# A hybrid Mamba, attention and FFN layer on eight cores: half of the scan's input products on GpSimd, FFN weights through two buffers, attention weights read from unpacked arrays

## The reference

```python
x = x + mamba(layernorm(x))
x = x + ffn(layernorm(x))
x = x + attention(layernorm(x))
x = x + ffn(layernorm(x))          # the same FFN weights again

# mamba: 2048 inner channels d, 16 states n, 2048 steps t
xb, zb = silu(conv4(h @ Wx)), silu(h @ Wz)
dt, B, C = x_proj(xb); dt = softplus(dt @ dt_proj)
decay[t,d,n] = exp(dt[t,d] * A[d,n])
inp[t,d,n]   = dt[t,d] * B[t,n] * xb[t,d]
h[t] = decay[t] * h[t-1] + inp[t]
y[t,d] = sum_n h[t,d,n] * C[t,n]
out = ((y + xb * D) * zb) @ out_proj

# ffn: weights become alpha * sign(w), alpha = mean |w| of a row
# attention: for every token its 16 heads of 64 attend to one another, then Wo
```

## Time and profile before

| | |
|---|---|
| median of the 2 runs | 6503.46 us (6502.35 to 6504.58) |
| the profiled execution, its own time | 6548.37 us |
| span of that execution, slowest core (core 7) | 6546.8 us (6480.4 to 6546.8 over the cores) |
| TensorE busy in the span | 2947.1 us (45%) |
| VectorE busy | 3181.0 us (49%) |
| ScalarE busy | 1508.9 us (23%) |
| GpSimd busy | 351.3 us (5%) |

### The profile page before, as it was taken

One profiled execution on the slowest core, in us unless ns is written; L12 is line 12 of the kernel. 1 busy time (PEld: TensorE's weight loads), 2 busy tenths in 40 slices (PEclk: granted clock), 3 DMA queues, 4 the chain that ended last, 5 costly groups with the idle time before them and its releaser, 6 DMA issues.

```text
span 6546.8 us, 37208 instructions; the slowest of 8 cores (6480.4 to 6546.8 us)
## 1 busy us (share of the span) xinstructions
PE 2947.1 (45%) x10144; PEld 1174.4 (18%) x10144; DVE 3181.0 (49%) x2980; ACT 1508.9 (23%) x2890; POOL 351.3 (5%) x204
## 2 busy tenths in 40 slices
PE   2323224322242322422224777879533443347978
PEld 1100001000010000100001444534211111113433
DVE  0267783577845778558885000010355556552011
ACT  1133331233322333223332222221100010001120
POOL 0000000000000000000000000000022222220000
PEclk9655557655575555665556666778766666668989
DMA  5300003100010000110001112211200000001213
GB/s 111 81 12 10 2 0 77 36 12 5 0 52 34 11 8 0 39 39 0 0 0 37 53 58 77 90 49 62 51 0 0 0 0 0 0 0 37 74 49 111
DMA packets 88973, 209.50 MB, mean 32 GB/s; under 512 B 32314, under 2 KB 32445, under 8 KB 83776
## 3 DMA queue, kind: packets, MB, share of 16 engines
q1 hardware_dynamic: 71584, 159.75, 7.6%
q0 software_dynamic: 17184, 47.37, 3.5%
HBM read 191.40 MB, written 37.88 MB: 35 GB/s over the span
## 4 chain that ended last, share of the span: by engine, by line
DVE 34%; PE 34%; ACT 11%; issue 9%; DMA 5%; DVEq 4%; ACTq 2%; POOL 1%; SPq 0%; POOLq 0%
DVE AR L739 18%; PE ps L982 8%; PE ps L1065 8%; ACT AR L717 5%; DVE AR L1213 4%; PE ps L478 3%; DVEq L58 3%; DVE AR L1249 3%; PE ps L1276 2%; DVE AR L519 2%; PE ps L314 2%; PE ps L1180 2%; PE ps L960 2%; ACTq L58 1%; POOL AR L1262 1%
## 5 line engine op out<-in xcount | busy, mean ns | idle before, releaser
L763 PE MATMUL ps<-AR 128*128 128x512 bf16 x1024 | 517.8, 608 | 1939.9 <-DVE AR L755 1939.9
L739 DVE TENSOR_TENSOR_SCAN AR<-AR 128x1024 bf16<-128x1024 f32 x512 | 1173.3, 2292 | 135.9 <-ACT AR L723 124.6
L1082 DVE TENSOR_SCALAR AR<-ps,AR 128x1024 f32<-128x1024 f32 x32 | 43.0, 1344 | 1333.3 <-ACT AR L1077 684.5
L717 ACT ACTIVATE AR<-AR 128x511 f32<-128x511 f32 x1024 | 675.4, 707 | 1.4 <-issue 1.1
L982 PE MATMUL ps<-AR 128*128 128x512 bf16 x2048 | 552.8, 441 | 84.2 <-DVE AR L349 84.2
L1276 PE MATMUL ps<-AR 128*128 128x512 bf16 x512 | 220.2, 586 | 635.8 <-POOL AR L1262 609.2
L1065 PE MATMUL ps<-AR 128*128 128x512 bf16 x2048 | 497.8, 410 | 4.7 <-ACT AR L994 4.7
L763 PEld LDWEIGHTS ps<-AR 128*128 128x128 bf16 x1024 | 70.2, 104 | 2379.0 <-issue 2379.0
L748 ACT ACTIVATE AR<-AR 128x2 f32<-128x2 bf16 x512 | 105.3, 206 | 1351.3 <-DVEq L63 1351.3
L755 DVE TENSOR_TENSOR AR<-AR 128x1024 bf16<-128x1024 bf16 x512 | 354.2, 692 | 125.4 <-issue 125.4
L478 PE MATMUL ps<-AR 128*128 128x512 bf16 x1024 | 308.7, 464 | 149.3 <-DVE AR L349 66.1
(11 more groups left out here) (102 smaller groups left out, 2559.4 us busy)
## 6 DMA issues: line engine op xcount, KB each, us to landing
AR<-ip_bf SPq DMA_DIRECT2D x96, 256.0 KB, 2.6
AR<-w2s SPq DMA_DIRECT2D x48, 512.0 KB, 3.6
AR<-bc_hbm SPq DMA_DIRECT2D x4, 4096.0 KB, 14.3
AR<-w2pk SPq DMA_DIRECT2D x16, 1024.0 KB, 6.2
AR<-op_bf SPq DMA_DIRECT2D x24, 512.0 KB, 3.6
AR<-w1s SPq DMA_DIRECT2D x48, 256.0 KB, 2.6
AR<-w1s POOLq DMA_DIRECT2D x48, 256.0 KB, 2.9
X<-x_fm SPq DMA_DIRECT2D x1, 8192.0 KB, 29.6
```

Source lines behind the costliest of these rows:

```text
L717: nbase=nbase: e.activation(out=dec_all[gb][:, n, 1:TQ], in_=dt[b][:, 1:TQ], func=AF.Exp, scale=av[:, dd, nbase + n:nbase + n + 1]))
L739: e.tensor_tensor_scan(out=h_all[hb].rearrange("p a b -> p (a b)"), data0=dec_all[gb].rearrange("p a b -> p (a b)"), data1=inp_all[ib].rea ...
L763: e.matmul(self.bank(b, TQ), self.ident[:], hc_all[hb][:, n, :], start=(ng == 0 and n == 0), stop=(ng == NG - 1 and n == G - 1)),
```

## The change

There are three parts.

**Scan.** For odd ng the input product no longer runs on VectorE but on GpSimd (new line 735; for even ng it stays on VectorE, new line 744). GpSimd waits for the scan of group ng-2 (its output buffer is that scan's input) and for vdup; VectorE's scan of the odd group waits for GpSimd's event in addition to ScalarE's. The prologue's write of vdup waits for the last GpSimd product that read it, and SP waits for GpSimd before it loads B and C.

**FFN.** The first product's weights go through two buffers instead of four and are all issued by SP.

**Attention.** Wq, Wk, Wv and Wo are read from the plain transposed matrices with a rearranged view instead of from packed arrays.

```diff
                     r.wait("ve", "d_spb", bc_done)
-                    r.op("ve", lambda e, b=b, ib=ib, nbase=nbase:
-                         e.tensor_tensor(
-                             out=inp_all[ib][:, :, 1:],
-                             in0=vdup[b][:, :, 1:],
-                             in1=bbc[:, nbase:nbase + G, 1:],
-                             op=ALU.mult))
-                    r.drain("ve")
+                    if ng % 2 == 1:
+                        if dd + ng > 0:
+                            r.wait("gp", "c_ve", h_done.get(keyp2, 0))
+                        r.wait("gp", "c_ve", vv[b])
+                        r.wait("gp", "d_spb", bc_done)
+                        gi = r.op("gp", lambda e, b=b, ib=ib, nbase=nbase:
+                                  e.tensor_tensor(
+                                      out=inp_all[ib][:, :, 1:],
+                                      in0=vdup[b][:, :, 1:],
+                                      in1=bbc[:, nbase:nbase + G, 1:],
+                                      op=ALU.mult), inc="c_gp")["c_gp"]
+                        gp_last[b] = gi
+                        r.wait("ve", "c_gp", gi)
+                    else:
+                        r.op("ve", lambda e, b=b, ib=ib, nbase=nbase:
+                             e.tensor_tensor(
+                                 out=inp_all[ib][:, :, 1:],
+                                 in0=vdup[b][:, :, 1:],
+                                 in1=bbc[:, nbase:nbase + G, 1:],
+                                 op=ALU.mult))
+                        r.drain("ve")
                     r.wait("ve", "c_act", col0_done)
...
             for m in range(32):
                 b = m % 2
-                B = m % 4
-                q = "sp" if m % 2 == 0 else "gp"
-                pb = (m // 2) % 2
-                sem = dsem(q, pb)
-                if m >= 4:
-                    r.wait(q, "c_pe", mm_done[m - 4])
+                if m >= 2:
+                    r.wait("sp", "c_pe", mm_done[m - 2])
...
-                    ddone = r.op(q, lambda e, m=m, B=B: e.dma_start(
-                        out=w1b[B].rearrange("p a b -> p (a b)"),
+                    ddone = r.op("sp", lambda e, m=m, b=b: e.dma_start(
+                        out=w1b[b].rearrange("p a b -> p (a b)"),
                         in_=d["w1s"][m * 128:(m + 1) * 128, :]),
...
-        for i, wname in enumerate(("wqpk", "wkpk", "wvpk")):
+        for i, wname in enumerate(("wqT", "wkT", "wvT")):
             r.op("gp", lambda e, i=i, wname=wname, wq=wq, wk=wk, wv=wv:
-                 e.dma_start(out=(wq, wk, wv)[i]
-                             .rearrange("p a b -> p (a b)"),
-                             in_=d[wname]),
+                 e.dma_start(out=(wq, wk, wv)[i],
+                             in_=d[wname].rearrange("(k p) f -> p k f", p=128)),
...
             ddone = r.op("gp", lambda e, m=m, b=b: e.dma_start(
-                out=wb[b].rearrange("p a b -> p (a b)"),
-                in_=d["wopk"][m * 128:(m + 1) * 128, :]),
+                out=wb[b], in_=d["woT"][:, m * 128:(m + 1) * 128]
+                .rearrange("(k p) f -> p k f", p=128)),
```

More of the change, by code:

```diff
@@ L557, in do_xproj @@
             r.wait("sp", "c_ve")
+            r.wait("sp", "c_gp")
             r.wait("sp", "d_spb")
@@ L631, in do_scan @@
             dt_ev = [0, 0]
+            gp_last = [0, 0]
             vv = [0, 0]
@@ L671, in prologue @@
                 r.wait("ve", "d_spb", bc_done)
+                r.wait("ve", "c_gp", gp_last[b])
                 r.op("ve", lambda e, dd=dd, b=b: e.tensor_tensor(
@@ L913, in _ffn @@
         w1b = [self.view(o_w1 + i * 8 * 128 * 2, BF16, [128, 8, 128])
-               for i in range(4)]
+               for i in (0, 1)]
         w2h = [self.view(o_w2 + i * 16 * 128 * 2, BF16, [128, 16, 128])
@@ L944, in _ffn @@
                 if prep:
-                    if st_done[B]:
-                        r.wait(q, sem, st_done[B])
-                    ddone = r.op(q, lambda e, m=m, B=B: e.dma_start(
-                        out=sg1[B].rearrange("p a b -> p (a b)"),
+                    if st_done[b]:
+                        r.wait("sp", dsem("sp", b), st_done[b])
+                    ddone = r.op("sp", lambda e, m=m, b=b: e.dma_start(
+                        out=sg1[b].rearrange("p a b -> p (a b)"),
                         in_=d["w1pk"][m * 128:(m + 1) * 128, :]),
-                         inc=sem, inck=16)[sem]
@@ L951, in _ffn @@
-                    r.wait("act", sem, ddone)
-                    r.op("act", lambda e, B=B: e.sign(out=w1b[B],
-                                                      in_=sg1[B]))
+                         inc=dsem("sp", b), inck=16)[dsem("sp", b)]
+                    r.wait("act", dsem("sp", b), ddone)
+                    if st_done[b]:
+                        r.wait("act", dsem("sp", b), st_done[b])
+                    r.op("act", lambda e, b=b: e.sign(out=w1b[b],
+                                                      in_=sg1[b]))
@@ L954, in _ffn @@
                     r.drain("act")
[L955 to L958, removed]
+                    r.op("act", lambda e, b=b: e.activation(
+                        out=sg1[b], in_=sg1[b], func=AF.Abs))
+                    ab_done[b] = r.inc("act", "c_act")
+                    r.wait("pe", "c_act", ab_done[b])
@@ L959, in _ffn @@
                     for k in range(8):
-                        r.op("pe", lambda e, m=m, B=B, k=k: e.matmul(
-                            self.bank(0, 512)[:, m:m + 1], sg1[B][:, k, :],
+                        r.op("pe", lambda e, m=m, b=b, k=k: e.matmul(
+                            self.bank(0, 512)[:, m:m + 1], sg1[b][:, k, :],
                             self.onesf[:, 0:1], start=(k == 0),
                             stop=(k == 7)))
-                    r.wait(q, "c_act", ab_done[B])
-                    st_done[B] = r.op(
-                        q, lambda e, m=m, B=B: e.dma_start(
+                    r.wait("sp", "c_act", ab_done[b])
@@ L973, in _ffn @@
                         in_=d["w1s"][m * 128:(m + 1) * 128, :]),
-                         inc=sem, inck=16)[sem]
-                    r.wait("pe", sem, ddone)
+                         inc=dsem("sp", b), inck=16)[dsem("sp", b)]
+                    r.wait("pe", dsem("sp", b), ddone)
                 if m >= 2:
@@ L980, in _ffn @@
                     for k in range(8):
-                        c = r.op("pe", lambda e, m=m, b=b, B=B, k=k, a=a,
-                                 bnd=bnd: e.matmul(
+                        c = r.op("pe", lambda e, m=m, b=b, k=k, a=a, bnd=bnd:
+                                 e.matmul(
                                      self.pair(4 + 2 * b, TH)[:, a:bnd],
-                                     w1b[B][:, k, :], xn[:, k, a:bnd],
+                                     w1b[b][:, k, :], xn[:, k, a:bnd],
                                      start=(k == 0), stop=(k == 7)),
@@ L1389, in make_in_maps @@
         "woT": np.ascontiguousarray(inputs["L0_attn_b_Wo"].T),
-        "wopk": np.ascontiguousarray(
-            inputs["L0_attn_b_Wo"].T.reshape(8, 128, 8, 128)
-            .transpose(2, 1, 0, 3).reshape(1024, 1024)),
         "bqkv": np.stack([inputs["L0_attn_b_bq"], inputs["L0_attn_b_bk"],
```

30 lines of the change are left out of this document (9 added, 21 removed).

## The result

The changed kernel takes 6871.72 us (median of 11 runs), the kernel before 6503.94 us (10 runs). The ratio is 1.0561, 95% interval 1.0534 to 1.0588: some 365 us more, where 298 were forecast. Three slow runs of the changed kernel (6933 to 7002 us), in which the cores of one die ran at a lower granted clock than the others and took longer, are left out of the ratio. The profiled execution has a span of 6851.0 us on its slowest core, core 1.

The account below looks back on a forecast made before the run. ScalarE's chain, not VectorE's product, was taken to bound the scan, with a period of 4.10 us. The forecast added 294 us for the scan and 4 us for loads and stray waits: 298 us, 6503 to 6801 us, range 6650 to 6980.

Parts of the forecast that it names:

- The bound: Scan: it waits for ScalarE's chain, not the product; period 4.10 us, so removing the product gains 0, at most 40 us.
- Rival 5: Scan: VectorE was the bound after all and 40 us come back, 6463 us; chance 2%.
- Exclusion and its place: Scan: GpSimd's product and VectorE's two-SBUF-input instructions exclude each other; GpSimd runs behind L755, delaying the even group's product; 294 us.
- Rival 2: Scan: back-to-back VectorE keeps GpSimd out until it waits at the odd scan; 188 us more, 6695 us; chance 17%.
- Rival 1: Scan: GpSimd comes ahead of L755 (h*C), also late at a block's end; 420 us more, 6923 us; chance 18%.
- The delay of a pair: Scan: each of 192 pairs of groups has its even scan start 1.53 us later (P - 0.37).
- P: Scan: duration of GpSimd's product, taken as 1.90 us, in proportion to the attention's 3.67 us for 2048 elements.
- 192 pairs: Scan: three of four GpSimd products per channel block cause a delay, 3 x 64; the fourth costs nothing.
- FFN and attention: Weight loads outside the scan: FFN loads hidden, 0; 4 us for the first Wo load and stray FFN waits.
- a line between two other loads: Attention: Wo's 1024 pieces put at 6.5 us, between 3.8 us (128 pieces) and 9.6 us (2048 pieces).

Follow-up runs that it names:

- the product under the scan: Kernel before with the scan part, GpSimd's product also waiting for the seed copy of the even group before, so it comes just behind that scan's start: ratio 1.0358.
- the fill: Kernel before with the scan part, GpSimd filling the odd group's input columns with a constant instead of the product, same waits and output: ratio 0.9991.

## Why the prediction was right, point by point

**The bound.** Right, and shown by leaving the work out: the product was not on the path, ScalarE's carry copy, Exp and seed copy were. Rival 5 had VectorE as the bound and gave back 40 us; the kernel without the odd products, for which a VectorE bound would mean as much as 146 us, was not faster at all.

**Exclusion and its place.** Right: L768 first, GpSimd behind it, the even group's product behind GpSimd. Rival 2 expected that VectorE, issuing back to back, keeps GpSimd out until it has to wait for it. It does not: L744 started at 522.18, 0.08 us before L768's end, and GpSimd, waiting since 521.68, was let in between the two. In every row shown here and in the earlier trace rows the instruction that started first was served first, and L744 started after GpSimd. Rival 1 is what happens in nine of the 256 products on this core. That the exclusion holds for the scan is shown by the product under the scan. That a GpSimd instruction which reads nothing does not exclude VectorE is shown by the fill; that the reading is the cause was argued from it, since the fill is also shorter and another operation.

The place was right by a small margin, and the reason given for it was thin. The prediction set GpSimd's wake in the attention, 0.15 us, against VectorE's 0.10. Counted from the scan's end, 0.15 would have put GpSimd ahead of h*C at 0.24, which is rival 1. What the trace has is 0.35 us for GpSimd (median of the three products of a block on core 1) against 0.24 for h*C. That fits a wake of 0.15 counted from the event, which the prediction's rival 1 saw out by 0.18. A margin of 0.11 us decided it, and where h*C came at 0.59 instead, the order turned. That part of the right answer is luck.

**The sizes.** The delay of a pair was set at 1.53 us and is 1.78. The term that was too small is GpSimd's product: P was taken as 1.90 us, in proportion to the attention's 2048 elements, and the product alone takes 2.11 to 2.12 us (the row at 543.06). Behind L768 it takes 1.98 instead of 1.76. The estimate that was worked out from the Trainium skill ("GPSIMD Engine Reference", section 3.1), 2.6 cycles per element and so 2.2 us, was nearer: 2.12 us are 2.5 cycles of 1.2 GHz per element. The proportion failed since the attention's product runs at 3.67 us for 2048 elements, 1.79 ns each, against 2.07 ns here; there both inputs are broadcast views, and whether that is the reason was not tried. The other 0.05 us is the step from a product to the scan, 0.15 instead of 0.10. 192 x 1.78 = 342. Over its 192 pairs, the seven turned ones included, core 1 lost 343.7 us; the rest of its scan changed by less than 3 us in any part, and 342.0 us remain from the first scan to the last.

**What the sum left.** The ratio says 365 us, the profiled pair 348 on core 1. The lowest runs of the two kernels, 6500.49 and 6846.47 us, lie 346 us apart, which agrees with the traces. The runs that the ratio compares spread from 6846 to 6923 us after the change and from 6500 to 6517 before, and the remaining 19 us lie within that spread; none of the experiments takes them apart.

**FFN and attention.** Right: 3.7 us on core 1 in the profiled pair, no more than cores of equal clock differ among themselves (2955.4 to 2960.2 us on the eight cores after, 2955.6 to 2958.6 on cores 0 to 3 before). The load of w1s through two buffers was always in time but for 2.1 us. Wq, Wk and Wv landed a little earlier than the packed ones, 35.4 instead of 37.6 us. Wo's 1024 pieces cost 0.6 us in landing (4.4 us against 3.8) and not the 2.7 that a line between two other loads gave.

## What to carry to other kernels

Before work is moved off a busy engine, follow the wait that ends last in one period of the loop: here a copy of 0.2 us in another engine's program order held the period, and changing its place was worth more than the offload. What an engine is busy with is not what it is held up by, and work left out in an experiment tells the two apart in one run. In the rows shown, a GpSimd product and a VectorE instruction with two inputs in SBUF, a scan included, never ran side by side: one of the two stood still until the other was done. A GpSimd fill ran beside such instructions for nothing, and so did a GpSimd product beside a VectorE instruction with one input in PSUM. So the price of a product moved to GpSimd was GpSimd's duration, 1.98 us, and not the 0.69 us that it took on VectorE.

## What had not been expected

That GpSimd gets the memory between two VectorE instructions which are issued back to back (0.08 us apart the wrong way) had been given 45%; here it is what happens in 185 of 192 pairs. A GpSimd fill of 1022 bf16 elements takes 0.95 us and disturbs nothing. A drain and a separate semaphore instruction behind a scan cost 0.24 us before the next instruction, a drain with the event on the scan itself 0.16. And a load of 1024 short pieces takes GpSimd's queue 0.88 us to issue, where the packed one took 0.53.
